# Conv-attention hybrid: the sums of the last two token blocks and the expert output at the turn between images, and the first stage in the order of its needs

## The reference

```python
# layer 0, on xn = group norm of x (32 groups)
q, k, v = Wq xn + bq, Wk xn + bk, Wv xn + bv
out = softmax(q^T k) v                                # 2304 x 2304 per image
se  = sigmoid(relu(mean(xn) @ w1.T) @ w2.T)           # squeeze-excite
x   = x + gamma * out + xn * se
# layer 1, on tokens t = x^T (2304 x 128)
t = t + softmax(tn tn^T) tn                           # tn = layer norm of t
p = softmax(u router_w + router_b)                    # u = layer norm of t; 8 experts, top 2, renormalised
t = t + sum over the two chosen experts of p_e * (u expert_w[e] + expert_b[e])
```

## Time and profile before

| | us |
|---|---|
| median of 3 runs | 2839.08 (2837.59 to 2839.95) |
| the profiled execution | 2836.02 |
| its span | 2834.2 |
| TensorE busy | 2636.5 (93%) |
| VectorE busy | 2161.3 (76%) |
| ScalarE busy | 2023.1 (71%) |
| GpSimd busy | 446.9 (16%) |

### The profile page before, as it was taken

How to read it: one execution, slowest core, us unless ns; L and a number is a source line. 1 busy time by engine, 2 the same in 40 slices (tenths; PEclk the granted TensorE clock), 3 DMA queues, 4 the chain that set the end, 5 groups by cost and what they waited for, 6 DMA issues and landing times.

```text
span 2834.2 us, 45738 instructions
## 1 busy us (share of the span) xinstructions
PE 2636.5 (93%) x15334; PEld 2381.2 (84%) x15334; DVE 2161.3 (76%) x5499; ACT 2023.1 (71%) x4305; POOL 446.9 (16%) x840
## 2 busy tenths in 40 slices
PE   5999989999899998999989999999999999999996
PEld 4888978889788897889978898888988889888895
DVE  4886778787787877877778777887777877788775
ACT  2777767677676876768767687676867768677774
POOL 0000210032100331003200133001220022200223
PEclk7999999999999999999999999999999999999997
DMA  1000000000000000000000000000000000000000
GB/s 35 1 1 18 7 6 1 18 7 6 7 1 18 7 6 7 1 18 7 9 4 1 18 7 11 2 1 18 10 9 1 1 21 6 9 1 1 4 9 12
DMA packets 10037, 23.05 MB, mean 8 GB/s; under 512 B 1992, under 2 KB 8528, under 8 KB 8784
## 3 DMA queue, kind: packets, MB, share of 16 engines
q1 hardware_dynamic: 9808, 20.14, 2.0%
HBM read 10.70 MB, written 9.44 MB: 7 GB/s over the span
## 4 chain that ended last, share of the span: by engine, by line
PE 61%; DVE 23%; ACT 9%; issue 5%; POOL 2%; SPq 0%; DMA 0%; ACTq 0%; DVEq 0%; POOLq 0%
PE ps L1005 17%; PE ps L1007 17%; PE ps L1006 17%; PE ps L1018 9%; DVE mx L818 6%; DVE pt_lo L828 3%; DVE pt_lo L902 3%; ACT pt_hi L612 2%; ACT p_rows L600 2%; DVE u_tok L879 1%; ACT p_rows L647 1%; POOL u_rs L518 1%; ACT pt_hi L656 1%; ACT p_rows L681 1%; DVE acc L984 1%
## 5 line engine op out<-in xcount | busy, mean ns | idle before, releaser
L612 ACT ACTIVATE pt_hi<-ps 128x384 fp32r<-128x384 f32 x864 | 425.4, 492 | 319.2 <-PE ps L1018 313.5
L828 DVE TENSOR_TENSOR pt_lo<-ps,pt_hi 128x384 fp32r<-128x384 f32 x864 | 479.5, 556 | 178.7 <-ACT pt_hi L612 170.3
L600 ACT ACTIVATE p_rows<-ps,negmax 128x512 f32<-128x512 f32 (+1 forms) x720 | 464.8, 647 | 72.9 <-DVE negmax L822 65.8
L902 DVE TENSOR_TENSOR pt_lo<-p_rows,pt_hi 128x768 fp32r<-128x768 f32 x432 | 413.9, 959 | 124.1 <-ACT pt_hi L656 122.4
L818 DVE TENSOR_REDUCE mx<-ps 128x1 f32<-128x512 f32 (+1 forms) x720 | 442.0, 633 | 79.4 <-PE ps L1007 55.4
L1018 PE MATMUL ps<-ident,p_rows 128*128 128x128 f32 x2736 | 455.7, 275 | 40.4 <-DVE pt_lo L828 22.9
L647 ACT ACTIVATE p_rows<-ps,shift 128x768 f32<-128x768 f32 x432 | 389.6, 902 | 119.1 <-PE ps L1007 114.0
L1018 PEld LDWEIGHTS ps<-ident,p_rows 128*128 128x128 f32 x2736 | 332.4, 140 | 153.8 <-issue 54.9
L656 ACT ACTIVATE pt_hi<-p_rows 128x768 fp32r<-128x768 f32 x432 | 365.6, 846 | 40.1 <-PE ps L1007 0.7
L1005 PE MATMUL ps<-pt_hi,v_hi 128*128 128x384 f32 x864 | 358.6, 415 | 2.5 <-ACT y_out L621 2.5
L1005 PE MATMUL ps<-xt_hi 128*128 128x384 f32 x864 | 305.2, 353 | 0.0
(11 more groups left out here) (165 smaller groups left out, 5162.4 us busy)
## 6 DMA issues: line engine op xcount, KB each, us to landing
x_chan<-x SPq DMA_DIRECT2D x8, 1152.0 KB, 5.1
y<-y_out SPq DMA_DIRECT2D x48, 192.0 KB, 1.9
p_rows<-ew SPq DMA_DIRECT2D x1, 512.0 KB
p_rows<-eb SPq DMA_DIRECT2D x1, 512.0 KB
p_rows<-wq SPq DMA_DIRECT2D x1, 64.0 KB
p_rows<-wk SPq DMA_DIRECT2D x1, 64.0 KB
p_rows<-wv SPq DMA_DIRECT2D x1, 64.0 KB
w_sb<-w SPq DMA_DIRECT2D x2, 4.0 KB
```

The lines of the kernel that those rows point to most:

```text
L600: act.activation(p_rows[:, ROW_BUFFER[r, n % 2], a:a + w], ps[:, c, 0:w], ACT.Exp, bias=negmax[:, r % 2:r % 2 + 1], accum_out=dparts[:, n, ...
L612: act.activation(pt_hi[:, slot, :], ring_bank(step)[:, 0:BW], ACT.Copy)\
L828: dve.tensor_tensor(pt_lo[:, slot, :], ring_bank(step)[:, 0:BW], pt_hi[:, slot, :], ALU.subtract).then_inc(pt_lo_ready, 1)
L902: dve.tensor_tensor(p1_lo[:, w % 3, :], p1_f[:, w % 2, :], p1_hi[:, w % 3, :], ALU.subtract).then_inc(p1_lo_ready, 1)
```

## The change

1. **At the turn**, o1t is split into the transposes (`o1t`) and the sums (`o1add`). With a next image, o1t of block 4 goes to end + 3 and of block 5 to end + 6, o1add of block 4 directly behind row 0's `row_max` (end + 4) and of block 5 behind row 1's (end + 10). Where o1t stood in the ring, waits for its bank are now waits for o1add.
2. **After the last image**, o1t and o1add of blocks 4 and 5 stand at end + 2 and end + 3, and the experts of both start six slots earlier. `moe` takes the slot of ut as an argument, with the same values as before.
3. **The first stage**: x comes in three loads with a semaphore each, the other 13 loads become 5, in the order x part 0, the three projection weights, x parts 1 and 2, the channel biases, the squeeze-excite weights, the expert biases, the expert weights. ScalarE makes w_hi. Each engine waits for what a step needs. The plan goes statistics, then xgnorm, xg and kproj interleaved by third; squeeze-excite, vproj, base and the bias fold (as steps `fold` and `foldsplit` in the ring) stand between the scores of rows 0 to 2. The fold's buffers move from p_rows to t_tok, the ones to t_late. Later images also load x in three parts.

```diff
+def first_stage():
+    s = statistics(0)[:9]
+    s += [("xgnorm", 0, 0), ("xg", 0, 0), ("xgnorm", 0, 1), ("kproj", 0, 0), ("xg", 0, 1), ("kproj", 0, 1), ("xgnorm", 0, 2),
+          ("kproj", 0, 2), ("xg", 0, 2), ("qproj", 0, 0), ("kproj", 0, 3), ("kproj", 0, 4), ("kproj", 0, 5)]
+    rest = {1: [("gn_norm", 0)], 2: [("se_in", 0)], 3: [("se_out", 0)], 5: [("fold", 0, 0)], 7: [("fold", 0, 1), ("base", 0, 0)],
+            9: [("fold", 0, 2)], 11: [("foldsplit", 0)], 13: [("base", 0, 1)], 15: [("base", 0, 2)]}
+    merge(rest, {slot: [("vproj", 0, m)] for m, slot in enumerate([0, 2, 4, 8, 12, 16])})
+    merge(rest, {j: attention0(0, 0, j) for j in range(NT)})
+    return s + [step for j in range(NT) for step in rest[j]]
...
-    for m, slot in enumerate([20, 29, 38, 46, end + 8, end + 11]):
-        merge(beside, {slot: [("o1t", b, m)]})
+    for m, slot in enumerate([20, 29, 38, 46]):
+        merge(beside, {slot: [("o1t", b, m), ("o1add", b, m)]})
     if b + 1 < B:
+        merge(beside, {end + 3: [("o1t", b, 4)], end + 6: [("o1t", b, 5)]})
         merge(beside, {end + j: attention0(b + 1, 0, j) for j in range(NT)})
+        for m, slot in ((4, end + 4), (5, end + 10)):
+            at = beside[slot].index(("row_max", b + 1, 0, m - 4)) + 1
+            beside[slot].insert(at, ("o1add", b, m))
     else:
-        merge(beside, moe(b, 4, end + 9, range(end + 14, end + 20), end + 21))
-        merge(beside, moe(b, 5, end + 17, range(end + 22, end + 28), end + 29))
+        merge(beside, {end + 2: [("o1t", b, 4), ("o1add", b, 4)], end + 3: [("o1t", b, 5), ("o1add", b, 5)]})
+        merge(beside, moe(b, 4, end + 3, end + 5, range(end + 8, end + 14), end + 15))
+        merge(beside, moe(b, 5, end + 11, end + 13, range(end + 16, end + 22), end + 23))
...
+            load(0, 0)
+            sp.dma_start(w_stage[:, :, :], wqkv).then_inc(qkv_loaded, 16)
+            load(0, 1)
+            load(0, 2)
+            sp.dma_start(biases[:, 0:4], channel).then_inc(biases_loaded, 16)
+            sp.dma_start(se_sb[:, :], se).then_inc(se_loaded, 16)
+            sp.dma_start(fold_b, eb).then_inc(fold_loaded, 16)
+            sp.dma_start(fold_w, ew).then_inc(fold_loaded, 16)
...
+                elif kind == "foldsplit":
+                    act.wait_ge(bias_folded, 1)
+                    act.activation(rw_pair[:, 0, :], rw_stage, ACT.Copy).then_inc(e_hi_ready, 1)
+                    act.activation(ew_hi[:, :], ew_stage, ACT.Copy).then_inc(e_hi_ready, 1)
...
+                    if not b:
+                        dve.wait_ge(w_hi_ready, 1)
+                        dve.tensor_tensor(w_lo[:, :, :], w_stage, w_hi[:, :, :], ALU.subtract).then_inc(w_lo_ready, 1)
+                        dve.wait_ge(biases_loaded, 16)
+                        dve.tensor_tensor(biases[:, 4:5], biases[:, 2:3], biases[:, 3:4], ALU.mult).then_inc(w_lo_ready, 1)
+                elif kind == "fold":
+                    a, z = FOLD_PARTS[step[2]]
+                    dve.wait_ge(ring_full, filled(step))
+                    dve.tensor_tensor(fold_b[:, a:z], fold_b[:, a:z], ring_bank(step)[:, 0:z - a], ALU.subtract)\
+                        .then_inc(bias_left, 1)
+                elif kind == "foldsplit":
+                    dve.wait_ge(bias_left, len(FOLD_PARTS))
+                    dve.scalar_tensor_tensor(out=fold_w, in0=fold_b, scalar=1.0 / C, in1=fold_w, op0=ALU.mult,
+                                             op1=ALU.add).then_inc(bias_folded, 1)
+                    dve.wait_ge(e_hi_ready, 2)
+                    dve.tensor_tensor(rw_pair[:, 1, :], rw_stage, rw_pair[:, 0, :], ALU.subtract).then_inc(e_split, 1)
+                    dve.tensor_tensor(ew_lo[:, :], ew_stage, ew_hi[:, :], ALU.subtract).then_inc(e_split, 1)
...
+                    if u == 0:
+                        dve.wait_ge(gn_rstd_ready, at(gn_rstd_ready, "gn_var", b))
...
-                elif kind == "o1t":
-                    m = step[2]
-                    dve.wait_ge(ring_full, filled(step))
-                    link(dve.tensor_reduce(r1[:, 0, :], tiled(ring_bank(step)[:, 0:BW]), AX.X, ALU.add))
+                elif kind == "o1add":
+                    m = step[2]
+                    bank = ring_bank(("o1t", b, m))
+                    dve.wait_ge(ring_full, filled(("o1t", b, m)))
+                    link(dve.tensor_reduce(r1[:, 0, :], tiled(bank[:, 0:BW]), AX.X, ALU.add))
```

More of the change, by code:

```diff
@@ L176, in batch @@
     return s
[L179 removed]
+PLAN = first_stage() + [step for b in range(B) for step in batch(b)]
 RAISES = {
@@ L193 @@
     "s1": ["s1_done", "p1_exp_ready", "p1_hi_ready"], "p1low": ["p1_lo_ready"], "pv1": ["pv1_done"], "o1evac": ["o1_chan_ready"],
-    "o1t": ["ring_full", "o1_added"], "uln": ["u_var_ready", "u_rstd_ready"], "uapply": ["u_tok_ready"],
+    "o1t": ["ring_full"], "o1add": ["o1_added"], "uln": ["u_var_ready", "u_rstd_ready"], "uapply": ["u_tok_ready"],
     "ut": ["ring_full", "u_hi_ready", "u_lo_ready"],
@@ L204 @@
         "yt": "y_chan_ready"}
-CHAINED = {"stat": 1, "gn_dev": 2, "se_out": 6, "rowsum": 3, "ot": 2, "ln": 6, "o1t": 5, "uln": 6, "router": 11,
+CHAINED = {"stat": 1, "gn_dev": 2, "se_out": 6, "rowsum": 3, "ot": 2, "ln": 6, "o1add": 5, "uln": 6, "router": 11,
            "expert": 3, "scores": 1, "lnapply": 2, "uapply": 2}
@@ L459, in _ @@
                     sp.wait_ge(ring_full, filled(("baset", b, NB - 1)))
-                    sp.dma_start(x_chan[:, :], x[b + 1]).then_inc(x_loaded, 16)
+                    for u in range(LB):
+                        load(b + 1, u)
                 if b:
@@ L562, in take @@
                     act.wait_ge(ring_full, filled(step))
+                    if m == 0 and not b:
+                        act.wait_ge(e_split, 2)
                     if m == 0 and b:
                         act.wait_ge(expert_added, at(expert_added, "expert", b - 1, 3, TPB - 1))
-                        act.wait_ge(o1_added, at(o1_added, "o1t", b - 1, NB - 1))
+                        act.wait_ge(o1_added, at(o1_added, "o1add", b - 1, NB - 1))
                     act.activation(t_tok[:, TPB * m:TPB * (m + 1), :], tiled(ring_bank(step)[:, 0:BW]), ACT.Copy)\
@@ L856, in take @@
                     else:
-                        dve.wait_ge(o1_added, at(o1_added, "o1t", b, m))
+                        dve.wait_ge(o1_added, at(o1_added, "o1add", b, m))
                     for k in range(TPB):
@@ L997, in _ @@
             pe.wait_ge(consts_made, 12)
-            pe.wait_ge(w_loaded, 16 * N_WLOADS)
-            for i, (a, z) in enumerate(FOLD_PARTS):
-                pe.matmul(ps[:, i, 0:z - a], ones[:, :], fold_w[:, a:z], start=True, stop=True).then_inc(column_sums, 1)
-            pe.wait_ge(w_split, W_SPLITS)
             def three(out, lhs_hi, lhs_lo, rhs_hi, rhs_lo, start=True, stop=True):
@@ L1012, in wait_ring @@
                 if i >= 2:
-                    pe.wait_ge(signals[LAST[RING[i - 2][0]]], at(signals[LAST[RING[i - 2][0]]], *RING[i - 2]))
+                    kind, *rest = RING[i - 2]
+                    pe.wait_ge(signals[LAST[kind]], at(signals[LAST[kind]], {"o1t": "o1add"}.get(kind, kind), *rest))
             def transpose3(step, src):
@@ L1036, in take @@
                         .then_inc(ring_full, 1)
+                elif kind == "fold":
+                    a, z = FOLD_PARTS[step[2]]
+                    pe.wait_ge(fold_loaded, 32)
+                    wait_ring(step)
+                    pe.matmul(ring_bank(step)[:, 0:z - a], ones[:, :], fold_w[:, a:z], start=True, stop=True)\
+                        .then_inc(ring_full, 1)
                 elif kind == "se_in":
                     wait_ring(step)
+                    if not b:
+                        pe.wait_ge(se_loaded, 16)
                     pe.wait_ge(se_in_ready, at(se_in_ready, "gn_norm", b))
@@ L1054, in take @@
                     pe.wait_ge(xg_lo_ready, at(xg_lo_ready, "xg", b, m // 2))
+                    if not b and not m:
+                        pe.wait_ge(w_lo_ready, 1)
                     wait_ring(step)
@@ L1153, in take @@
                     m = step[2]
+                    if not b and not m:
+                        pe.wait_ge(e_split, 2)
                     pe.wait_ge(u_lo_ready, at(u_lo_ready, "ut", b, m))
```

116 lines of the change are left out of this document (46 added, 70 removed).

## The result

The changed kernel takes 2816.25 us (median of 4 runs, 2815.79 to 2816.65) against 2838.41 for the kernel before, measured beside it (4 runs, 2837.59 to 2839.95): ratio 0.9921 [0.9904, 0.9938], faster by 22.2 us. The forecast was 2810.9, with 2806 to 2816 as its own range and 2806 to 2820 with its rivals. The profiled execution took 2816.04, and the span went from 2834.2 to 2814.3, so the traces have 19.9 to explain.

What follows compares the result with a forecast made beforehand. The kernel was taken as TensorE-bound, the edit touching nine stops priced as latency chains: start 18.5, turns 7.8, end 1.9, sum 28.2, so 2839.1 - 28.2 = 2810.9 us. Own range 2806 to 2816, with R1, R2 and R3 to 2820.

Steps and rivals of the forecast that it cites:

- R1: Rival: half clock through the whole start, total gain 22.2 us, time 2816.9; chance 0.17.
- A1: Start, up to R: earlier loads and statistics bring R from 26.4 to 10.7 us, bounds 10.1 to 11.6.
- R: Start: the reciprocal root of the group variance, at 26.4 us before the change and forecast at 10.7.
- A2: Start, from R to row 0's first exp: 26.4 us instead of 35.0, first exp at 37.1.
- A: The whole start, to row 2's exp: gain of 18.5 us, stage ending at 54.0 instead of 72.58.
- A3: Start, rows 1 and 2: 16.9 us instead of 11.1 with the work they now carry, giving back 5.8.
- B: The seven turns between images: gain of 1.12 us each, 7.8 in all; bounds per turn 0 and 1.87.
- R3: Rival: in the turns the wait moves from VectorE to TensorE, B = 0, total gain 20.4, 2818.7 us; chance 0.11.
- C: The end, after the last image's second attention: earlier sums gain 1.9 us (0 to 3).

Runs made afterwards that it cites:

- run 5: The changed kernel again, unaltered, on another chip, for a second profile: 2814.78 us.
- run 9: The kernel of run 8 without the filling matmuls ahead of and between the first projections: 2793.99 us, ratio 0.9847 to the kernel before.
- run 1: The changed kernel with the turn's order of transposes and sums undone, start and end as changed: 2816.02 us.
- run 3: The changed kernel with the transposes of blocks 4 and 5 behind the last scores of rows 0 and 1, nothing filled: 2804.47 us.
- runs 1 to 5: run 1, run 2, run 3, run 5, and the fourth: the changed kernel with both late transposes and filled gaps, 2798.27 us.
- run 2: The changed kernel with six unused 512-column matmuls behind the last scores of each of an image's first three rows: 2802.03 us.
- run 6: The kernel before, filled with the same six unused matmuls as run 2: 2828.16 us, ratio 0.9961 to the kernel before.
- run 10: run 9 with block 5's last transposes and sums moved behind block 4's uapply, and fourteen end filling matmuls placed elsewhere instead of eighteen: 2794.15 us.
- run 8: The changed kernel with late transposes and unused matmuls in TensorE's longer gaps in start, turns and end, also before and between first projections: 2794.98 us.
- run 7: The changed kernel with image 0's x in one load of 1152 KB instead of three: 2815.05 us (one run).

## Why the prediction was right, and where not

The measured 2816.25 lies inside the range of 2806 to 2820, at the upper edge of the forecast's own 2806 to 2816. The start and the end came as worked out, and the turns did not. The measured gain of 22.2 is that of R1 to the digit, which is chance: R1 had half clock in rows 1 and 2 of the start and 7.8 from the turns, and neither came.

**A1, R at 10.7**: it was 11.61, at the late end of its bounds (10.1 to 11.6), 11.07 in run 5 and 12.52 in run 9, where x's third part was there only at 8.30, later than the bound of 7.4. The four statistics of x's second and third part wait for the second until 6.38, where the line through two sizes had it at 5.2, so that line is too early for parts issued in a row. The 2.0 us of the fixed part in the Trainium skill (DMA: Bandwidth & Descriptors, section Anatomy of one DMA), by which the third part would have landed at 5.9 (an estimate), moves the forecast further from this trace: the last statistics ended at 8.42 (6.38 + 2.04). The table load went to 0.78, earlier than the 4 forecast; a likely reason, not shown, is that ScalarE's first instruction now waits for a DMA only. As forecast, it costs nothing.

**A2, 26.4 from R to the first exp**: it was 24.4. The order and the waits are as walked through; the clock was not. Scores matmuls start 0.43 apart until about 29.5 and 0.23 from 30.2 on, so more than half of row 0 ran at full clock where I had it at half. Where the clock rises in the start is luck. In traces with this same start it was up at about 23 us (run 1) and only at 36 (run 3), and R to the first exp took 22.2 to 27.0; in run 3, with nearly all of row 0 at half clock as I had assumed it, 27.0 against my 26.4. Row 2's negmax then stands between 50.59 (run 5) and 55.37 (run 3), so A is 17 to 22, around the forecast.

**A3, rows 1 and 2 at 16.9**: 7.27 + 9.72 = 17.0, and within 0.05 the same in runs 1 to 5. The two misses ahead of it (0.9 late, 2.0 early) give A = 19.6 instead of 18.5. What I had at nothing is the half-clock stretch behind the start, 1.6; with it A is 18.0.

**B, 7 x 1.12 = 7.8**: brought 0.1. The mechanism is there: VectorE has no sums between row 1's maxima, o1t 5 waits 0.24, the interval is 6.44 where I had 6.4. At full clock the turn gains 7.76 - 6.44 - 0.45 = 0.87 by the traces of the two kernels (I had row 0 later by 0.25 only), and 0.94 by runs 2 and 6. So about a fifth of the 1.12 was never there. The step that failed is the sentence that clock dips "can come and go", with one dip read off as noise common to both orders. They are no noise of that kind. They follow TensorE's stop in the turn, which both orders have (2.50 before, 2.04 after), and they go when it is filled (1.14 and 0.69). In the old order row 1 was limited by VectorE's sums, and part of the half clock was covered: it cost 0.35 to 1.3 in a first interval, 1.3 where it fell ahead of the sums. Taking the sums out made TensorE the limit, so the half clock is paid in full, 1.3 to 1.6 in a first interval, in five turns of seven, six in the repetition. Another 1.3 each is paid in row 2, in three turns instead of two. I had written this as a width of 2.5, not as a loss that the edit exposes. Two runs show it from both sides: undoing the order changes nothing (run 1), holding the clock up brings 14 us (run 2). How much of the change's gain the clock took is less sure than that it did: 14.2 less the 11.0 of the kernel before is 3.2 by the medians, 14.5 less 6.9 is 7.6 by the profiled executions. In total this is R3's result, B near 0, by another cause than R3's: o1t 5 waits 0.24, and row 1's scores start 2.36 behind row 0's negmax instead of 2.05.

The Trainium skill (TensorE: Matmul & The Clock Gate, section A second HAM failure mode) tells of short TensorE stops that make the clock swing. I weighed it for the start alone, where half clock through rows 1 and 2 (R1) did not come. Its place was the turns: there the trace agrees, with 2.04 us of stop, 2 us of full speed and then 3.4 us at 0.50 in the turn into image 2. The turns into images 1 and 6 have the same stop and stay at full clock.

**C, 1.9**: 1.87, in the steps forecast. In run 10 about half of the 2.4 given away by having both sums ahead came back; GpSimd's order held back most of the rest.

**Sum**: 28.2 forecast, 19.9 in the spans (20.0 by terms): A +1.1 and then -1.6, B -7.7, C 0. That the sum stayed in range is owed to its width and to A and C, not to B. The measured medians are 22.2 apart; the profiled execution of before was 2.4 below the median of its four runs, that of after 0.2, and this is the 2.2 between the two accounts.

**Still open**: which of the turns fall to half clock, with a stop of 2.04 in each; why row 2 never does in run 3; and by how much the start of the best version could still be shortened, since the early filling moved the half clock instead of removing it.

## What to carry to other kernels

Where an edit takes another engine's work out of a row of matmuls, ask what TensorE's clock is in that row after its last stop: if TensorE becomes the limit, half clock that was covered is paid in full, and it can eat the whole gain. Price the gain at both clocks. A stop of some 2 us in an otherwise dense stream can be tried out cheaply by issuing a few matmuls of no use in it, in its own gap, behind the work that others wait for and never ahead of it.

## What the runs showed of the hardware

- A TensorE that had been busy for hundreds of us at full clock stopped for 2.04 us, and 1.9 us after it resumed it ran 3.4 us at half clock, though it was 100% busy by then (windows of turn 2). With a stop of 2.04 this happened in five of seven turns (six in run 5), with 2.50 in four (kernel before; a fifth had it behind row 2), with the stop at 1.14 (run 6) or 0.69 (run 2) in none of seven. Six matmuls, 1.55 us together, behind each of an image's first three rows made 14 us in the changed kernel and 11 in the kernel before.
- Filling that comes too early moves the half clock: in run 8 it lay on 24 to 40 us, with TensorE 100% busy in both windows shown of that stretch.
- The granted clock in the profile's windows can be off: in the start of after it says 1.00 from 8 to 30 us, also from 26 to 30 with TensorE 100% busy, while matmuls of 512 columns start 0.43 apart there until 29.5, as they do at 0.50 elsewhere. The distance of the matmuls is the safer reading.
- Three loads of 384 KB issued together are reported with a median of 4.7 us to landing, against 5.1 for one of 1152 KB: the first is usable at 4.2, the second at 6.4, the last before 7.4 (4.18, 5.58 and 6.85 in run 5; 4.27, 5.63 and 8.30 in run 9). The one load of 1152 KB of run 7 was usable at 6.20.
